# Start of the loads, late clearing, and a closing product of zeros in a transformer block

## What is computed

```
x = x + attention(layernorm(x))     # 16 heads of 8 channels, causal, w_qkv, w_proj, biases
x = x + ffn(layernorm(x))
# ffn: 8 experts, each relu(x W1[e] + b1[e]) W2[e] + b2[e], hidden 512,
# summed with weights p * (p > 0.5), p = sigmoid(x Wg + bg); all experts run on all tokens
```

## Time and profile before

| | us |
|---|---|
| median of 3 runs | 677.46 (677.27 to 679.45) |
| profiled execution, own time | 677.06 |
| its span | 675.3 |
| TensorE busy | 652.4 |
| mean granted TensorE clock | 0.977 |

### The profile page before, as it was taken

The page is one execution under the profiler, slowest core; times in us unless marked ns, Lnnn a source line. Parts: engine busy times, 40 slices in busy tenths (PEclk is TensorE's granted clock), DMA queues, the critical chain, the costliest instruction groups (busy, mean ns, idle before and its releaser), DMA issues.

```text
span 675.3 us, 12981 instructions
## 1 busy us (share of the span) xinstructions
PE 652.4 (97%) x4325; PEld 439.9 (65%) x4325; DVE 450.6 (67%) x1019; ACT 443.2 (66%) x857; POOL 339.1 (50%) x445
## 2 busy tenths in 40 slices
PE   4989998999999999999999999999999999999998
PEld 3445565667666766667666766666666766677776
DVE  6757786678676876678676876678576776344343
ACT  2446768667766776667776786667666667646543
POOL 5117444457545654457545654456645554554453
PEclk7958999999999999999999999999999999999999
DMA  5441224220322122220322122221322010100200
GB/s 178 97 138 23 57 47 110 58 57 19 92 64 57 48 58 57 73 57 25 93 56 59 48 58 58 73 58 34 79 54 50 31 34 33 49 33 33 79 31 17
DMA packets 24560, 40.08 MB, mean 59 GB/s; under 512 B 3312, under 2 KB 12920, under 8 KB 24496
## 3 DMA queue, kind: packets, MB, share of 16 engines
q1 hardware_dynamic: 24112, 38.89, 20.8%
q10 hardware_dynamic: 384, 0.38, 0.2%
HBM read 23.46 MB, written 2.23 MB: 38 GB/s over the span
## 4 chain that ended last, share of the span: by engine, by line
PE 90%; DVE 3%; ACT 2%; issue 1%; DMA 1%; POOL 1%; SPq 0%; ACTq 0%; DVEq 0%; POOLq 0%
PE ring L1273 11%; PE y_bank L1398 10%; PE ring L1353 10%; PE ring L1206 9%; PE ring L1208 9%; PE ring L1207 9%; PE y_bank L1405 9%; PE y_bank L1400 9%; PE ring L1280 4%; PE ring L1212 3%; DVE f_buf L1174 1%; PE ring L1295 1%; ACT xn L870 1%; PE ring L1369 1%; PE y_bank L1273 1%
## 5 line engine op out<-in xcount | busy, mean ns | idle before, releaser
L969 ACT ACTIVATE h_hi<-ring 128x512 fp32r<-128x512 f32 x256 | 152.6, 599 | 110.4 <-PE ring L1208 106.7
L937 ACT ACTIVATE pt<-ring 128x512 f32<-128x512 f32 x312 | 171.0, 599 | 53.0 <-PE ring L1273 51.1
L845 POOL TENSOR_TENSOR h_lo<-h_all,h_hi 128x512 fp32r<-128x512 f32 x96 | 123.6, 1288 | 161.4 <-ACT h_all L975 143.1
L1161 DVE SCALAR_TENSOR_TENSOR h_lo<-ring,h_hi 128x512 fp32r<-128x512 f32 x160 | 109.1, 685 | 57.1 <-ACT h_hi L969 57.1
L838 POOL TENSOR_SCALAR_AFFINE_SELECT pt<-pt 128x512 f32<-128x512 f32 x128 | 79.8, 637 | 94.5 <-ACT pt L937 94.3
L1094 DVE CUSTOM_DVE_ANT_0 ring<-causal,ring 128x512 f32<-128x512 bf16 x124 | 83.3, 713 | 51.8 <-PE ring L1273 51.8
L1398 PE MATMUL y_bank<-h_hi,w_lo 128*128 128x512 f32 x256 | 110.8, 433 | 2.7 <-DVE f_buf L1174 2.7
L1206 PE MATMUL ring<-x2T_lo,w_hi 128*128 128x512 f32 x256 | 101.9, 398 | 0.0
L1273 PE MATMUL ring<-stack 32*128 32x384 f32 (+3 forms) x998 | 97.1, 372 | 4.9 <-DMA stack<-nmT 2.9
L1208 PE MATMUL ring<-x2T_hi,w_hi 128*128 128x512 f32 x256 | 101.2, 395 | 0.0
L1400 PE MATMUL y_bank<-h_hi,w_hi 128*128 128x512 f32 x256 | 101.2, 395 | 0.0
(11 more groups left out here) (145 smaller groups left out, 795.8 us busy)
## 6 DMA issues: line engine op xcount, KB each, us to landing
f_buf<-gates SPq DMA_DIRECT2D x32, 512.0 KB, 3.7
stack<-parts SPq DMA_DIRECT2D x95, 128.0 KB
x_in<-in_x SPq DMA_DIRECT2D x8, 256.0 KB, 3.0
f_buf<-in_W SPq DMA_DIRECT2D x2, 1024.0 KB, 7.7
out_x<-f_buf SPq DMA_DIRECT2D x7, 256.0 KB, 2.4
stack<-nmT SPq DMA_DIRECT2D x64, 8.0 KB
stack<-stack SPq DMA_DIRECT2D x28, 16.0 KB
out_x<-f_buf SPq DMA_DIRECT2D x2, 128.0 KB, 1.9
```

The costliest lines, as they stand in the source:

```text
L845: g_.tensor_tensor(h_lo[:, (i * SLOTS + s) % H_RING, :], h_all[:], h_hi[:, (i * SLOTS + s) % H_RING, :].bitcast(F32), ALU.subtract).then_i ...
L937: sc.activation(pt[:, slot, :], b[:], ACT.Exp, scale=SCALE).then_inc(free_sem("ex", i, g, u), 1)
L969: sc.activation(h_hi[:, (i * SLOTS + s) % H_RING, :], bank_of("z", i, s)[:], ACT.Relu).then_inc(s_hhi, 1)
L1161: v.scalar_tensor_tensor(out=h_lo[:, (i * SLOTS + s) % H_RING, :], in0=bank_of("z", i, s)[:], scalar=0.0, in1=h_hi[:, (i * SLOTS + s) % H_ ...
```

## The change

1. ScalarE issues the three loads of b1 ahead of the load of the bias columns.
2. GpSimd's `stackset` (and the clearing of v that follows it) waits until VectorE has split b1 and the q and k weights.
3. W2's DMA is issued by ScalarE instead of SyncE.
4. A score visit that has no masks, and is followed by anything but a visit, `pv` or `warm`, ends with a bf16 product: identity by 8 columns of `causal` that are zero, added to the last unit's bank. That product raises the unit's semaphore.
5. `SHIFT` gets other values, and three costs of DMA items are changed, so that every engine's order may differ.

```diff
-SHIFT = {('act', 'exp', False): 23.0,
-         ('act', 'exp', True): 3.5,
-         ('act', 'nm', False): 15.0,
-         ('act', 'nm', True): -2.5,
-         ('dve', 'klo', False): 4,
-         ('dve', 'merge', False): 8,
-         ('dve', 'merge', True): -2,
-         ('dve', 'qlo', False): 3.0,
-         ('dve', 'smax', False): -4.5,
+SHIFT = {('act', 'exp', False): 25.5,
+         ('act', 'nm', False): 25.0,
+         ('act', 'nm', True): -4.5,
+         ('dve', 'hlo', False): -3,
+         ('dve', 'merge', False): 2,
+         ('dve', 'merge', True): -2.0,
+         ('dve', 'smax', False): -5.0,
...
-         ('dve', 'w1', False): 4.0,
-         ('dve', 'xT', False): 5.0,
-         ('dve', 'yT', True): 7.5,
+         ('dve', 'w1', False): 3.5,
+         ('dve', 'xT', False): 10.0,
          ('pe', 'ex', False): 3.0,
-         ('pe', 'ex', True): -11.5,
...
-         ('pe', 'max', False): 12.5,
+         ('pe', 'max', False): 17.0,
+         ('pe', 'max', True): 3.0,
...
+         ('pe', 'q', True): 6,
...
-         ('pe', 'w1', False): 0.5,
+         ('pe', 'w1', False): 6.0,
...
-         ('pool', 'nm', False): 10.5}
+         ('pool', 'causal', False): -4,
+         ('pool', 'causal', True): 9.5}
...
-    put("dma", ("b1", None), -60.5, 600, ("dma", ("wqkv", None)))
-    put("dma", ("w1", 0), -60, 2500, ("dma", ("b1", None)))
+    put("dma", ("b1", None), -60.5, 1200, ("dma", ("wqkv", None)))
+    put("dma", ("w1", 0), -60, 1900, ("dma", ("b1", None)))
...
-    put("sp", ("w2load", None), -8.9, 600, ("pe", ("w1", EXPERTS - 1)))
-    put("dma", ("w2", None), -8, 9000, ("sp", ("w2load", None)))
+    put("act", ("w2load", None), -8.9, 700, ("pe", ("w1", EXPERTS - 1)))
+    put("dma", ("w2", None), -8, 9000, ("act", ("w2load", None)))
...
-    put("pool", ("stackset", 1), -20, 2200, ("pool", ("rs1", 0)))
+    put("pool", ("stackset", 1), -20, 2200, ("pool", ("rs1", 0)), ("dve", ("wqk", None)))
...
                 elif kind == "stackset":
+                    pool.wait_ge(s_wset, 6)
+                    pool.wait_ge(s_b1, 5)
                     g_.memset(stack_half(1), 1.0).then_inc(s_stackset, 1)
...
             act.dma_start(wqkv_in[:], w_qkv).then_inc(s_wqkv, 16)
-            act.dma_start(b_cols[:], b_cols_in).then_inc(s_bcols, 16)
             act.wait_ge(s_b1zero, 1)
             for k in range(3):
                 act.dma_start(b1_in[32 * k:32 * k + EXPERTS, :], b1).then_inc(s_b1load, 16)
+            act.dma_start(b_cols[:], b_cols_in).then_inc(s_bcols, 16)
...
-            def scores(mx, ex):
+            def scores(mx, ex, after):
...
+                masked = [("max", unit) for unit in mx if masked_by_pe(unit)]
+                zeros = not masked and after not in ("S", "pv", "warm")
+                if zeros:
+                    masked.append(units[-1][:2])
...
-                        stop = k == len(pieces) - 1 and not (kind == "max" and masked_by_pe(unit))
+                        stop = k == len(pieces) - 1 and (kind, unit) not in masked
...
+                if zeros:
+                    mm(bank_of(units[-1][0], *units[-1][1])[:, 0:8], ident16[:], causal[:, 0:8],
+                       start=False, stop=True,
+                       skip_group_check=True).then_inc(full_sem(units[-1][0], *units[-1][1]), 1)
```

More of the change, by code:

```diff
@@ L698, in _ @@
                                      rows[M_ROW + 4::M_STEP, :, 0, :]).then_inc(s_stack[g], 16)
[L699 to L702, removed]
                 elif kind == "mrow":
@@ L884, in _ @@
                     sc.activation(w1_hi[:, i * T:(i + 1) * T], b[:], ACT.Copy).then_inc(s_w1hi, 1)
+                elif kind == "w2load":
+                    act.wait_ge(*full("w1", EXPERTS - 1))
+                    act.dma_start(w2_in[:].rearrange("p a (c d) -> p (a c) d", d=C),
+                                 w2.rearrange("e (c p) d -> p (e c) d", p=P)).then_inc(s_w2, 16)
                 elif kind == "w2":
@@ L1283, in _ @@
             warmed = False
-            for w in ORDER["pe"]:
+            for w, after in zip(ORDER["pe"], [*ORDER["pe"][1:], ("end",)]):
                 kind = w[0]
@@ L1287, in _ @@
                 if kind == "S":
-                    scores(w[1], w[2])
+                    scores(w[1], w[2], after[0])
                     continue
```

## The result

| | before | changed |
|---|---|---|
| median, us | 677.68 (12 runs, 676.84 to 681.19) | 675.0 (12 runs, 674.2 to 676.5) |
| ratio to before | | 0.9954, interval 0.9938 to 0.9970 |
| span of the profiled execution | 675.3 | 672.6 |
| products of zeros, fillers, in TensorE's list | 0, 84 | 59, 110 |

What follows compares the result with a forecast made beforehand. TensorE was taken as the bound in program order, with loose time in the head. Terms -3.0 - 0.3 - 2.8 + 1.0 = -5.1 us gave 672.2 us, between 672.0 and 672.4; range 665.5 to 676.8.

Steps and rivals of the forecast that it cites:

- the clock: Head: with TensorE's hole before the W1 product gone, the clock may rise sooner; 0.3 us gained, bounds 0 and 0.65.
- part 5: All engines' lists: new due times reorder the same work; taken as 0, bounds -3 and +3 us.
- part 3: Head, before first exp scores: W2 issued by ScalarE lets the maxima land sooner; 2.8 us gained, bounds 0 and 2.9.
- rival B: Head: W2's traffic still delays the maxima from either queue, so only the clearing counts; 675.2 us, chance 0.15.
- Parts 1 and 2: Head: b1 issued 0.36 us earlier, its cast freed from GpSimd's memsets; first W1 product 3.0 us earlier, near 11.0.
- the cap: Head: TensorE's own transposes and fillers, ending at 10.93 us, limit how early the W1 product starts.
- one of the signs of being wrong: Head: the maxima landing 7 us after their copy would show the forecast wrong.
- Part 4: Unmasked score visit endings: 60 products of zeros cost 0.015 us each, about +1.0 us; bounds +9 and -4.8.
- Rival A's first half: Unmasked visit endings: the fp32 load hides behind the bf16 product, -4.8 us instead of +1.0, 666.4; whole rival's chance 0.20.
- Rival C: Even stretch: ScalarE's copy of the maxima, due 10 slots later, comes late and stalls TensorE; 684.6 us, chance 0.10.

Runs made afterwards that it cites:

- early_clearing: Changed kernel without GpSimd's two waits ahead of the clearing, lists unchanged: median 679.88 us, ratio 1.0022 to the kernel before.
- before_late_clearing: Kernel before with one edit, GpSimd's two waits ahead of the clearing: median 673.35 us, ratio 0.9937 to the kernel before.
- w2_on_sync: Changed kernel with W2 issued by SyncE ahead of the maxima, as before: median 676.23 us, ratio 0.9980 to the kernel before.
- no_zeros: Changed kernel without the 59 closing products of zeros, lists unchanged: median 673.63 us, ratio 0.9942 to the kernel before.
- zeros_256: Changed kernel with 256 columns instead of 8 in each closing product of zeros: total 672.48 us, ratio 0.9937 to the kernel before.

## Why the prediction came out as it did

The direction was right, the time lay in the range, and the sum was 5.1 us where 2.7 were found. Three of its terms were off. Two of the errors cancelled, the clock's 2.2 us too little and the 2.25 that part 5 put at nothing; that is luck. What is left is part 3. The time itself, 675.0, is rival B's 675.2, and of B's reasons the one on W2 came true.

**Parts 1 and 2** (3.0 us): right, mechanism and size. The cast took 0.42, the memsets started at 12.21, the W1 product came 3.10 us earlier, and early_clearing and before_late_clearing show it from both sides. b1's order was worth 0.39 us, near its low bound of 0.36. Only the cap was misread: TensorE's transposes and fillers ended at 10.45 and not at 10.93, which held at the lower clock, so the product waited 0.51 us for VectorE's steps.

**The clock** (0.3 us, bound 0.65): mis-sized. First scores came 5.63 us earlier, 2.5 more than the W1 product. I had argued how much sooner the clock would *return*. In this execution it did not *fall*: the 9.50 us of work between 9.6 and 19.8 ran at 1.00, where the kernel before had 0.50. Without these 2.5 us the other terms of the sum below come to -0.2: nearly all of the measured gain is this.

That the missing hole kept the clock up is not shown. Before, the clock fell at 9.6, ahead of the hole, which began at 10.93. The transposes at that place, with TensorE's idle time ahead of them, in the kernel before, early_clearing, w2_on_sync and the changed kernel:

```profile
9.49 1.02 PE L1212 MATMUL ring<-ident,xn 128*128 128x128 f32 x4 [1.92 <-ACT xn L870]
9.83 1.09 PE L1211 MATMUL ring<-ident,xn 128*128 128x128 f32 x4 [2.23 <-ACT xn L865]
9.79 0.96 PE L1219 MATMUL ring<-ident,xn 128*128 128x128 f32 x4 [2.03 <-ACT xn L873]
9.60 0.63 PE L1213 MATMUL ring<-ident,xn 128*128 128x128 f32 x4 [1.45 <-ACT xn L867]
```

In the first three the clock fell at 9.6 to 9.9. In the two that have the hole it stayed low up to 19.8; in w2_on_sync, without the hole, up to 13.3. So whether it falls there differs between executions, and the hole goes with how long it stays low. Over all executions the late clearing does lower the time at the lower level: its median is 20.1 with it and 31.1 without in the kernel before, 20.2 and 24.4 in the changed one. What decides the fall stays open.

**Part 3** (2.8 us): the step that failed. I read the blocked issue of 3.37 as the cost, and gave the small DMAs a flight of 2 to 3.2 us beside W2. The flight with W2 in the other queue is 6.55 us; with W2 held back it is 1.68. The maxima landed 7.2 us behind the copy, which was one of the signs of being wrong. The gain was 0.2 us, and w2_on_sync against the changed kernel gives 0.3. That was rival B, and its evidence was in the prediction: the transfer had taken 4.0 us even after the issue had ended. The Trainium skill (DMA: Bandwidth & Descriptors, "Issuing engines are not separate DMA queues") had the right word here, that another issuing engine saves issue time only; from the first issue to the landing it was 7.35 us before and 7.2 after, which agrees. In all eight profiled executions with W2 ahead in the other queue the flight was 6.3 to 6.6 us.

**Part 4** (+1.0 us): right: 0.87 to 0.96 us for the 47 products in the even stretch, and some 0.2 for the other 12 at the same rate, by no_zeros and the distance between z products. Each costs 0.0185 us where I had 0.015. zeros_256 fits the reading that the value came from, the bf16 load and not its columns. Rival A's first half is refuted. The Trainium skill's floor of 25 ns (TensorE: Matmul & The Clock Gate, "Wait — 56ns, not 53.3ns?") would have given, as an estimate, 1.18 us for 47 products; 0.87 to 0.96 were measured. The rows do not go below that floor, with 0.04 us from the product of zeros (125.12) to the next (125.16); what it added to the path is less.

**Part 5** (0, bounds -3 and +3): it was +2.25, nearly all of it in fillers of the head. The bound of +3 held, but the term was put at nothing without counting the fillers of the new list, 110 against 84. Rival C did not come: the even stretch is as full as it was (504.91 of 508.00 us, before 504.98), though ScalarE's copy of the maxima has its later due time.

-3.10 - 2.5 - 0.2 + 2.25 + 0.96 = -2.6; the stretch from the first to the 17th z product is 0.11 shorter: -2.7.

## What to carry to other kernels

When a small DMA waits beside a large one, ask when the large one starts, not who issues it; here 2 MB issued 5 us later gave what another queue did not, though ScalarE then waited 2.5 us for them. Where the granted clock changes within a kernel, price a hole in the work by what the clock does around it as well, and filler work by the time at which the clock falls without it; and look at many executions before a gain is put down to the clock. A scheduler's fillers show up as busy time, so count them apart before calling an engine full.

## What the runs showed of the hardware

- A VectorE bf16 cast of 0.42 us took 3.09 and 3.96 us beside GpSimd memsets of 1.81, 0.21, 1.81 and twice 0.2 us: in both it ended inside the last two, so it was held through several of them, not through one. VectorE's subtractions from a PSUM bank were not slowed by the same memsets: 0.63 and 0.69 us at 12.07 and 12.94 in the changed kernel, and 0.68 at 34.88 and 25.37 with GpSimd idle.
- The maxima's DMAs of 8 KB beside W2's 2 MB, issued 2.7 us behind them: the flight was 6.3 to 6.6 us when W2 stood in the other queue (eight executions), and 3.9 to 4.0 behind an issue of 3.4 in the same queue (three); with W2 held back it was 1.7 (two). That the large DMA causes the delay is shown by holding it back; how it does so is not.
- The lower clock level comes and goes differently in executions of the same kernel: all 12 executions of the changed kernel spend about 17.5, 20.2 or 24.3 us at it, and their spans follow (672.3 to 672.9, 673.2 to 674.4, 674.5 to 674.7). About half of the spread of the medians in the table is this (13.4 us, 7.4 in the last column), and a kernel's profiled execution may be a lucky one: 666.3 for W2 behind the maxima, where others had up to 672.7.
- In the changed kernel the clock was at its lower level through 17 us in which TensorE was busy 15.75, and at its higher one through the 10.2 us from 9.6, in which it was busy 9.50. What distinguishes the two stretches was not tried.
